# Cross heads: two of each group's 32 row maxima copied out by ScalarE and folded by GpSimd, three in the first group with the score pair's banks as their place

## The reference, cut to what matters

```python
attn = jax.nn.softmax(scores, axis=-1)       # scores: 4 x 16 x 512 x 1601, scaled, rotary, masked
out = jnp.einsum('bhqk,bhkd->bhqd', attn, V)
out = out.transpose(0, 2, 1, 3).reshape(b, sq, E)
return out @ Wo.T + bo
```

## Time and profile before

| | |
|---|---|
| median of three runs | 1865.03 us (1862.22 to 1865.31) |
| the profiled execution: its time | 1862.25 us |
| its span, first to last instruction | 1860.4 us |
| granted TensorE clock, mean | 0.959 of full speed |
| busy: TensorE, VectorE, ScalarE, GpSimd | 1700.7, 1362.3, 1041.6, 676.6 us |
| row maxima of the cross heads on VectorE (L2114) | 512 reductions, 984 ns the median of one, from 1175.4 to 1692.9 us |
| exponentials of the cross heads on ScalarE (L2102) | 288 pairs and 272 singles |

### The profile page before, as it was taken

One profiled execution on the slowest core, in us unless ns is written; L12 is line 12 of the kernel. 1 busy time (PEld: TensorE's weight loads), 2 busy tenths in 40 slices (PEclk: granted clock), 3 DMA queues, 4 the chain that ended last, 5 costly groups with the idle time before them and its releaser, 6 DMA issues. The chain is left out here.

```text
span 1860.4 us, 33962 instructions
## 1 busy us (share of the span) xinstructions
PE 1700.7 (91%) x13150; PEld 933.5 (50%) x13150; DVE 1362.3 (73%) x2346; ACT 1041.6 (56%) x1744; POOL 676.6 (36%) x756
## 2 busy tenths in 40 slices
PE   8999899979999998789999888599999999999996
PEld 4788577748888887433333555112222222222564
DVE  1533688856666666767777488989999999995764
ACT  1221565616655655236667343178888888887552
POOL 0555877224444443333341224314241212111453
PEclk9999999979999999869999999689999999999998
DMA  5044799958777774531110467412210101000001
GB/s 195 26 135 153 281 317 321 305 211 313 292 269 291 300 290 163 165 103 32 32 33 14 147 188 205 115 38 68 74 27 19 37 19 37 19 19 1 24 12 34
DMA packets 114101, 247.59 MB, mean 133 GB/s; under 512 B 28251, under 2 KB 83071, under 8 KB 110337
## 3 DMA queue, kind: packets, MB, share of 16 engines
q1 hardware_dynamic: 87652, 208.21, 32.3%
q0 software_dynamic: 24176, 35.12, 7.1%
q10 hardware_dynamic: 2112, 2.10, 0.3%
HBM read 183.39 MB, written 61.38 MB: 132 GB/s over the span
## 5 line engine op out<-in xcount | busy, mean ns | idle before, releaser
L2114 DVE TENSOR_REDUCE Eh_maxima<-Eh_max 128x2 f32<-128x802 f32 x512 | 474.6, 987 | 19.0 <-PE Eh_max L1993 13.8
L2102 ACT ACTIVATE Eh_probs<-Eh_pair 128x1024 f32<-128x1024 f32 (+1 forms) x288 | 287.5, 998 | 112.2 <-PE Eh_pair L2032 112.1
L1993 PE MATMUL Eh_max<-Eh_KS,Eh_QS 49*128 49x401 f16 x1024 | 196.8, 356 | 45.6 <-DVE Eh_maxima L2114 41.6
L1453 PE MATMUL C_y<-C_x_high,C_W 128*128 128x256 f16 (+1 forms) x1536 | 217.1, 254 | 8.8 <-ACT C_gate L1513 7.3
L2055 PE MATMUL Eh_av_ps<-Eh_probs,E_V 128*17 128x512 f32 (+1 forms) x1664 | 221.3, 604 | 0.0
L2114 DVE TENSOR_REDUCE Dh_maxima<-Dh_max 128x2 f32<-128x1024 f32 x128 | 152.0, 1221 | 43.9 <-PE Dh_max L2001 42.0
L1453 PE MATMUL C_y<-C_x_low,C_W 128*128 128x256 f16 (+1 forms) x768 | 181.6, 254 | 0.0
L2102 ACT ACTIVATE Eh_probs<-Eh_single 128x512 f32<-128x512 f32 x272 | 161.7, 595 | 25.4 <-PE Eh_single L2032 25.3
L1993 PEld LDWEIGHTS Eh_max<-Eh_KS,Eh_QS 49*128 49x128 f16 x1024 | 50.1, 94 | 232.8 <-DVE Eh_maxima L2114 200.2
L1831 POOL DMA_DIRECT2D Eh_KS<-E_kd x64 | 37.1, 580 | 350.9 <-PE Eh_pair L2032 346.1
L1453 PEld LDWEIGHTS C_y<-C_x_high,C_W 128*128 128x128 f16 x1536 | 139.7, 98 | 22.9 <-ACT C_gate L1513 9.5
(11 more groups left out here) (436 smaller groups left out, 3524.7 us busy)
## 6 DMA issues: line engine op xcount, KB each, us to landing
C_W<-w_split SPq DMA_DIRECT2D x24, 3072.0 KB
w_split<-B_w_parts SPq DMA_DIRECT2D x24, 768.0 KB, 8.4
Eh_KS<-E_kd POOLq DMA_DIRECT2D x64, 150.1 KB, 3.3
C_tail<-in_expert_tail_dram SPq DMA_DIRECT2D x24, 384.0 KB, 8.3
B_places<-in_w_experts_dram SPq DMA_DIRECT2D x10, 768.0 KB, 6.2
A_QT<-in_w_experts_dram SPq DMA_DIRECT2D x8, 768.0 KB, 5.0
w_split<-A_QT SPq DMA_DIRECT2D x8, 768.0 KB, 6.5
early_more<-in_w_experts_dram SPq DMA_DIRECT2D x8, 768.0 KB, 10.0
```

Source lines behind the costliest of these rows:

```text
L1453: last = mm(y_ps[n % Y_BANKS][:, i, 0:w], W[:, u, a, at_w:at_w + P], x[:, s % 2, k, 0:w], start=(q == 0), stop=(q == len(parts) - 1))
L1993: last = self.nc.tensor.matmul(bank[:, a, 0:self.cw], self.QS[r, slot, p, qt * P:(qt + 1) * P], self.KS[r, slot, p, k0:k0 + self.cw], star ...
L2102: self.nc.scalar.activation(dst, src, ACT.Exp, scale=1.0 / SCORE).then_inc(self.exp_done, 1)
L2114: self.nc.vector.tensor_reduce(self.maxima[:, g % 2, :, p * TPB + qt, c], self.max_ps[n % 2][:, :, 0:self.cw], AX_X, ALU.max).then_inc(sel ...
```

## The change

Two items of each group from 1 to 14 are no longer reduced by VectorE, those numbered 11 and 23, and three in group 0, those numbered 3, 11 and 19. Group 15 keeps all 32. For such an item

- TensorE fills the place as before. In group 0 it fills the pair of banks `pair_ps` for it, which no score needs yet, so that the other items keep both places of `max_ps`. In later groups the item takes its turn in `max_ps`, and the item two behind it waits for the copy.
- ScalarE copies 128 x 802 elements to SBUF (`keep_maxima`), at the item's place in the walk, behind the exponential of an earlier score.
- GpSimd folds them in three levels (`fold_maxima`), from 401 to 201, 101 and 51 columns, each level in three operations: left minus right, that or zero whichever is larger, plus right. That is the larger of the two.
- VectorE reduces what is left, 51 columns of all the group's items set aside, with one reduction ahead of the top (`rest_maxima`), after waiting for GpSimd.

The places for this are in XT for group 0 and in `HT_parts` for the later ones. GpSimd's order becomes: fold of the first item of group 0, the wait for the stores, load of group 1, the other two folds of group 0, load of group 2, and then for each g from 1: the folds of group g, the load of group g + 2 and the weights' work of g + 2. ScalarE's wait for the end of the stage before moves to just ahead of its first exponential.

```diff
+KEPT = 3
+ASIDES = ((3, 11, 19), (11, 23))
+FOLDED = (201, 101, 51)
...
+    def asides(self, g):
+        return (ASIDES[min(g, 1)] if g < GROUPS - 1 else ()) if self.keeping else ()
...
+    def bank_of(self, n):
+        if not self.keeping or n >= self.n_max:
+            return self.max_ps[(n - len(self.asides(0))) % 2]
+        return self.pair_ps if self.aside(n) else self.max_ps[(n - self.asides_before(n)) % 2]
...
+    def bank_free(self, pe, n):
+        if self.bank_before(n) >= 0:
+            self.item_done(pe, self.bank_before(n))
...
-        if n >= 2:
-            pe.wait_ge(self.read, n - 1)
-        bank, k0 = self.max_ps[n % 2], c * (self.cw - 1)
+        self.bank_free(pe, n)
+        bank, k0 = self.bank_of(n), c * (self.cw - 1)
...
+    def keep_maxima(self, act, n, m):
+        area, k = self.place_of(m)
+        act.wait_ge(self.filled, n + 1)
+        if k >= KEPT:
+            act.wait_ge(self.folded, 3 * (self.asides_before(m) - KEPT + 1))
+        self.nc.scalar.activation(self.keep[area][:, k % KEPT], self.bank_of(n)[:, :, 0:self.cw], ACT.Copy).then_inc(self.kept, 1)
+
+    def fold_maxima(self, pool, g, first=0, end=None):
+        for j, i in list(enumerate(self.asides(g)))[first:end]:
+            m = g * self.n_max + i
+            n, (area, k) = self.asides_before(m), self.place_of(m)
+            pool.wait_ge(self.kept, n + 1)
+            src, width = self.keep[area][:, k % KEPT], self.cw
+            for step, w in enumerate(FOLDED):
+                if step:
+                    pool.wait_ge(self.folded, 3 * n + step)
+                dst = self.fold[area][step] if step < 2 else self.rest[area][:, j]
+                left, right = src[:, :, 0:w], src[:, :, width - w:width]
+                self.nc.gpsimd.tensor_tensor(dst, left, right, ALU.subtract).then_inc(self.excess, 1)
+                pool.wait_ge(self.excess, 2 * (3 * n + step) + 1)
+                self.nc.gpsimd.tensor_scalar(dst, dst, 0.0, 0.0, ALU.max, ALU.add).then_inc(self.excess, 1)
+                pool.wait_ge(self.excess, 2 * (3 * n + step) + 2)
+                self.nc.gpsimd.tensor_tensor(dst, dst, right, ALU.add).then_inc(self.folded, 1)
+                src, width = dst, w
+
+    def rest_maxima(self, dve, g):
+        mine = self.asides(g)
+        first, step = mine[0] // self.chunks, (mine[1] - mine[0]) // self.chunks
+        end = mine[-1] // self.chunks + 1
+        dve.wait_ge(self.folded, 3 * self.asides_before((g + 1) * self.n_max))
+        self.nc.vector.tensor_reduce(self.maxima[:, g % 2, :, first:end:step, self.chunks - 1],
+                                     self.rest[g > 0][:, 0:len(mine)].rearrange("p j a w -> p a j w"), AX_X, ALU.max).then_inc(self.rest_ready, 1)
+        dve.wait_ge(self.rest_ready, g + 1)
...
+            if kind in "MB":
+                m = k[1] if kind == "B" else k
+                if self.aside(m):
+                    self.keep_maxima(act, n, m)
...
+        if not self.aside(m):
+            dve.wait_ge(self.filled, n + 1)
...
+        if self.asides(g):
+            self.rest_maxima(dve, g)
...
+                heads.fold_maxima(pool, 0, 0, 1)
                 places.all_stored(pool)
...
+                heads.load(pool, 1)
+                heads.fold_maxima(pool, 0, 1, 3)
+                heads.load(pool, 2)
+                for g in range(1, GROUPS):
+                    heads.fold_maxima(pool, g)
+                    if g + 2 < GROUPS:
+                        heads.load(pool, g + 2)
+                        beside.beside(pool, g + 2)
```

More of the change, by code:

```diff
@@ L1879, in __init__ @@
         self.row_loads = 16 * 2
+        self.keeping = not self.causal
+        self.counts = self.count_items()
+        if self.keeping:
+            self.kept, self.excess, self.folded, self.rest_ready = sem("kept"), sem("excess"), sem("folded"), sem("rest_ready")
+            widths = [KEPT * self.cw] + list(FOLDED[:-1]) + [len(ASIDES[0]) * FOLDED[-1]]
+            place = lambda area, i: area[:, 2 * sum(widths[:i]):2 * sum(widths[:i + 1])]
+            self.keep = [place(area, 0).rearrange("p (k a w) -> p k a w", a=2, w=self.cw) for area in self.start.spare_areas()]
+            self.fold = [[place(area, 1 + i).rearrange("p (a w) -> p a w", a=2) for i in range(2)] for area in self.start.spare_areas()]
+            self.rest = [place(area, 3).rearrange("p (j a w) -> p j a w", a=2, w=FOLDED[-1]) for area in self.start.spare_areas()]
@@ L1881, in turn_of, with aside, asides_before, count_items @@
     def turn_of(self, g):
         return g // self.slots + 1
+    def asides(self, g):
+        return (ASIDES[min(g, 1)] if g < GROUPS - 1 else ()) if self.keeping else ()
+    def aside(self, m):
+        g, i = divmod(m, self.n_max)
+        return i in self.asides(g)
+    def asides_before(self, m):
+        g, i = divmod(m, self.n_max)
+        return sum(len(self.asides(q)) for q in range(g)) + sum(j < i for j in self.asides(g))
+    def count_items(self):
+        counts = [(0, 0)]
+        for kind, k in self.walk():
+            if kind in "MBRT":
+                by_act = kind in "MB" and self.aside(k[1] if kind == "B" else k)
+                counts.append((counts[-1][0] + (not by_act), counts[-1][1] + by_act))
+        return counts
@@ new lines, in bank_of, with bank_before @@
+    def bank_of(self, n):
+        if not self.keeping or n >= self.n_max:
+            return self.max_ps[(n - len(self.asides(0))) % 2]
+        return self.pair_ps if self.aside(n) else self.max_ps[(n - self.asides_before(n)) % 2]
+    def bank_before(self, n):
+        if not self.keeping or n >= self.n_max:
+            return n - 2
+        same = [i for i in range(n) if self.aside(i) == self.aside(n)]
+        back = 1 if self.aside(n) else 2
+        return same[-back] if len(same) >= back else -1
@@ L2000, in bias_maxima @@
         for a in range(2):
-            last = self.nc.tensor.matmul(self.max_ps[n % 2][:, a, qt * P:(qt + 1) * P], self.ident_score[:], self.tri[:, 0, :], start=False, stop=True,
+            last = self.nc.tensor.matmul(self.bank_of(n)[:, a, qt * P:(qt + 1) * P], self.ident_score[:], self.tri[:, 0, :], start=False, stop=True,
                                          skip_group_check=True)
@@ L3037, in _, with ready @@
             def _(act):
+                def ready(act):
+                    act.wait_ge(low_ready, ITEMS)
+                    places.all_stored(act)
                 first_scalar(act)
-                act.wait_ge(low_ready, ITEMS)
-                places.all_stored(act)
-                heads.scalar(act)
+                heads.scalar(act, ready)
                 start.warm_up(act)
```

48 lines of the change are left out of this document (31 added, 17 removed).

## The result

The changed kernel takes 1906.56 us (median of 4 runs, 1902.33 to 1909.55) against 1865.17 us (1862.22 to 1865.42, 4 runs beside them) before: ratio 1.0214, 95% interval 1.0189 to 1.0239, some 41 us slower by the medians. The prediction said 1886, range 1856 to 1897: the direction is right, the size is half of what came. The profiled execution has a span of 1902.8 us, 42.4 longer than before.

What follows compares the result with a forecast made beforehand. TensorE and ScalarE were taken to set the pace through a step's middle up to M20, VectorE from there to its end. Terms: 12 x 0.96 = 11.5, + 11.2, - 1.6 = +21.1 us; median 1886, range 1856 to 1897.

Steps and rivals of the forecast that it cites:

- M5: Place of group item 11 in a regular step, said to lie ahead of where VectorE is late.
- M17: Place of group item 23 in a regular step, said to lie ahead of where VectorE is late.
- Rivals 1 and 2: Regular steps: the removed reductions come back, 1857 us, chance 0.20; or half comes back, 1868 us, chance 0.13.
- M20: Place in a step's order of maxima from which VectorE was said to set the pace to the end.
- M29: Maximum late in a step where TensorE waits 0.31 us for VectorE, read as VectorE being late.
- M21: Maximum in a step where TensorE waits 0.49 us for VectorE, read as VectorE being late.
- (a): M17 without its reduction: the 0.94 us are all waiting, and ScalarE's copy makes it +0.15 us per regular step.
- (b): M5 without its reduction: ScalarE's copy delays the exponential and the next score pair, +0.40 us per regular step.
- (c): VectorE's reduction of the rest, in front of the top, counted in full: +0.41 us per regular step.
- (d): GpSimd's folds, 6.1 us each: hidden in regular steps, late in the two steps with the weight split, together +11.2 us.
- (e): Start, before the first scores: three maxima leave VectorE, the folds end last by 0.6 us, first top -1.6 us.
- Rival 3: GpSimd's folds are slow, 8.05 us by a 0.30 gap, late in every step: +39.5 us, 1905, chance 0.07.

## Why the prediction was half of it

**The bound.** Right where it was used: M5 and M17 stand where TensorE and ScalarE set the pace. Taking both reductions away returned 0.09 us a step, and leaving the items out altogether 0.35, of 1.88. Rivals 1 and 2, which had the reductions or one of them come back, are out. The trace disagrees with the rule weighed in the prediction: 1.65 us less of VectorE's busy time a step returned 0.09. That rule is the Trainium skill's (Perfetto Trace Analysis, Identifying the Most-Contended Engine: the engine with the highest occupancy is the one to relieve). But the sentence that VectorE sets the pace from M20 on is wrong at least for M29, and for M1 behind it: items 3 and 7, read by nobody, gave 0.27 back of 1.88. I took the wait of 0.31 us at M29 for a bound; it was the later of two waits by a little. The wait of 0.49 us at M21, read the same way, was not tested.

**(a) and (b), the copies.** Forecast 0.15 + 0.40 = +0.55, measured +0.63 for the copies alone, with the larger part at item 11, as forecast. The 0.84 of one copy, taken in proportion between two rows, was measured as 0.84 and 0.85.

**(c), the rest.** 0.41 was forecast in full. After the copies only 0.21 is left of the step's +0.84. The operation lasts 0.36 us as forecast; that part of it is hidden, since VectorE is not what sets the pace, is likely and not shown. Regular step: +0.96 forecast, +0.84 measured, closer than its terms, because one came out above and one below.

**(d), the fold: the first step that failed.** The term mis-sized is the one-input operation: rows of other one-input operations, a multiplication by a constant and a cast, gave 530, 365 and 282 ns, and it is 1561, 895 and 561. A fold takes 7.7 us, not 6.1. The changed middle operation showed both halves of this: the price and its share of the split steps (3.7 and 3.6 us). Of 17.2 measured there, 7.3 is this, and 9.9 stands against the 11.2 of the forecast.

**(e), the start.** The same term: three folds in a row end 3 x 1.6 us late, and -1.6 became +3.3. With the cheap operation it was -2.3. Rival 3 had slow folds, for another reason (the gap, which stayed at 0.08), and its 1905 is near the result partly by chance: it counted 0.4 us a regular step that didn't come, and had no term for the clock.

**The clock: the second step that failed.** The prediction has no term for it: it took every step of the changed kernel at full clock, as the regular steps of before are, and gave no reason. In the changed kernel it falls to 0.50, the lower of its two levels, 1.2 GHz, in most steps (windows of 1 us in one of them):

```profile
1558.00:1559.00 1.00, 0.66 (x5) 0.12 (x3) 1.00 (x2) 1.00 (x2) 0.92 (x1) 1.00 0.00 0
1559.00:1560.00 1.00, 0.75 (x4) 0.13 (x4) 1.00 (x2) 0.66 (x2) 0.83 (x3) 0.59 0.00 0
1560.00:1561.00 1.00, 1.00 (x10) 0.15 (x8) 0.99 (x2) 0.77 (x1) 0.92 (x2) 0.50 0.00 0
```

A fall of about 3.4 us costs a step 1.0 to 1.4 us, some 9 us in all. In the steps without a weight split it begins 3.5 to 5.5 us ahead of the next top, among TensorE's waits at M21 to M23; in the split steps it also comes as TensorE stands behind the late folds, 1.5 or 1.6 us ahead of the top. It is no property of the folds, of the copies, or of more work: of the 14 steps behind the first, ten have it with no fold, six with items 11 and 23 read by nobody and ten with items 3 and 7 gone. What decides stays open: the same busy time ahead leads to a fall in one step and not in the next. In the kernel without items 3 and 7:

```profile
1494.50:1497.50 3.00, 1.90 (x17) 0.48 (x19) 3.00 (x4) 2.83 (x4) 0.00 (x0) 1.00 0.00 0
1497.50:1501.00 3.50, 3.50 (x21) 0.65 (x23) 2.44 (x4) 1.68 (x3) 0.00 (x0) 0.51 0.00 0
1527.50:1530.50 3.00, 1.90 (x16) 0.51 (x13) 3.00 (x5) 2.65 (x5) 0.00 (x0) 1.00 0.00 0
1530.50:1534.00 3.50, 3.50 (x29) 0.77 (x30) 3.38 (x4) 2.84 (x4) 0.00 (x0) 1.00 0.00 0
```

The kernel before has the same in its steps of 32.41, one of them here, and none of them falls:

```profile
1298.50:1301.50 3.00, 1.90 (x16) 0.45 (x13) 3.00 (x4) 2.93 (x4) 0.00 (x0) 1.00 0.85 350
1301.50:1304.50 3.00, 3.00 (x27) 0.55 (x23) 2.88 (x4) 2.34 (x4) 0.00 (x0) 1.00 0.00 0
```

Nor does any of the eleven steps of 32.41 in each of the two kernels that change group 0 alone. Every edit to the regular steps that was tried, the removal of work included, brought falls. So part of what an edit costs here is the falls that come with it. Only one execution of each kernel is traced; others of the kernel before took up to 1875.94 us with a mean clock down to 0.951 (0.959 in the traced one), so falls in its regular steps can't be excluded there. Whether it is the length of the step that matters was not shown.

## What to carry to other kernels

A wait in the timeline shows who was last, not what would be gained: before relieving an engine, look for the next wait behind it, and if it's cheap, leave the work out altogether once and time it; here that shows that little of it is to be had (0.35 of 1.88 us). Compare only steps that have no fall of the clock in them nor just before them. Price an operation from a row with the same arithmetic on the same engine, not only the same form and shape, and if there is none, keep both ends of the range well apart. Work moved to a queue that other work already holds costs the sum of the two wherever both meet.

## What the hardware showed that was not expected

- GpSimd's one-input operation with a maximum and an addition takes 1561, 895 and 561 ns at 402, 202 and 102 columns, and with a multiplication and an addition 532, 368 and 284: 3.3 against 0.8 ns a column ((1561 - 561) / 300 and (532 - 284) / 300).
- TensorE's clock falls for about 3.4 us in a stage where TensorE is busy over 90% of the time, behind stretches that in other steps leave it alone (busy 1.90 of 3.00 us in both). In the kernel whose items 11 and 23 nobody reads, three falls cost 4.09 us, and 0.57 of this stood in the full-clock step behind them.
- Leaving two of 32 items out of a step, TensorE's part included, left the time where it was (ratio 0.9998) or made it longer (1.0029).
